# Delta-rule groups: the second sweep of the solve's level one moves between the halves of the third projection, and VectorE's corner copy moves ahead of y's turn and the sum of squares

## The reference, cut to what matters

```python
qkvz = x @ W_qkvz                       # q, k, v, z of all heads
qkv = silu(causal_conv1d(q | k | v))    # four taps along the tokens
attn = -(k_beta @ k.T * decay_mask)     # strictly lower triangle, chunk by chunk
...                                     # row by row: attn becomes (1 - attn)^-1
value_corrected = attn @ v_beta
for c in chunks:
    v_prime = v_c - k_cumdecay_c @ state
    out     = (q_c @ state) * ge_c + intra_c @ v_prime
    state   = state * gel_c + (k_c * kd_c).T @ v_prime
core = rmsnorm(core * silu(z)); out = core @ W_out
```

## Time and profile before

| | |
|---|---|
| median of 3 runs | 1669.9 us (1666.23 to 1676.31) |
| the profiled execution | 1677.4 us, of which 1675.6 us is the span from first to last instruction |
| PE busy in the span | 84% |
| DVE, ACT, POOL busy | 69%, 49%, 47% |
| the delta rule's 16 groups | from about 560 us to 1550 us of the span |

### The profile page before, as it was taken

One profiled execution on the slowest core, in us unless ns is written; L12 is line 12 of the kernel. 1 busy time (PEld: TensorE's weight loads), 2 busy tenths in 40 slices (PEclk: granted clock), 3 DMA queues, 4 the chain that ended last, 5 costly groups with the idle time before them and its releaser, 6 DMA issues. The chain is left out here.

```text
span 1675.6 us, 38381 instructions
## 1 busy us (share of the span) xinstructions
PE 1406.2 (84%) x14345; PEld 999.1 (60%) x14345; DVE 1156.0 (69%) x2350; ACT 822.9 (49%) x2163; POOL 782.8 (47%) x1118
## 2 busy tenths in 40 slices
PE   5988994189545899999999999999999999976675
PEld 2543342066422567777777677777777777765465
DVE  6887126923475788888888788888887888833623
ACT  3334871043132466665665565665665666632122
POOL 5100000177213366467567467566566566543443
PEclk9999996589877999999999899999999999987788
DMA  8200005066723464565565464654555555331884
GB/s 280 74 2 2 2 1 157 1 199 211 256 58 66 114 148 122 149 177 125 160 156 131 128 160 122 162 153 144 139 157 148 119 160 148 99 107 57 241 253 130
DMA packets 249433, 218.72 MB, mean 131 GB/s; under 512 B 88770, under 2 KB 224962, under 8 KB 247200
## 3 DMA queue, kind: packets, MB, share of 16 engines
q1 hardware_dynamic: 234992, 192.41, 42.7%
q0 software_dynamic: 5712, 15.60, 2.8%
q10 hardware_dynamic: 8544, 8.26, 1.6%
HBM read 133.85 MB, written 82.25 MB: 129 GB/s over the span
## 5 line engine op out<-in xcount | busy, mean ns | idle before, releaser
L1825 DVE SCALAR_TENSOR_TENSOR d_conv<-d_big,all_cw,d_conv 128x1023 f32<-128x1023 f32 (+2 forms) x192 | 245.4, 1278 | 45.6 <-ACT d_conv L2067 43.6
L1547 PE MATMUL d_big<-all_xn_t,all_w 128*128 128x512 f32 x512 | 252.6, 624 | 18.7 <-DVE d_conv L1825 11.9
L1547 PEld LDWEIGHTS d_big<-all_xn_t,all_w 128*128 128x128 f32 x512 | 93.8, 198 | 101.4 <-issue 88.2
L2166 ACT COPY d_ys<-d_big 128x128 f32<-128x128 f32 x256 | 61.0, 266 | 177.7 <-PE d_big L1715 139.8
L2301 POOL TENSOR_TENSOR d_y<-d_y,all_xn 128x256 f32<-128x256 f32 x128 | 96.9, 757 | 107.3 <-DVE d_y L1977 89.5
L1753 PE MATMUL d_big<-all_wo,d_yt 128*128 128x256 f32 x512 | 125.5, 391 | 13.8 <-DVE d_yt L1902 13.8
L2258 POOL TENSOR_TENSOR d_vs<-d_vs,d_sv 128x1024 f32<-128x1024 f32 x32 | 61.2, 1912 | 135.6 <-DMA d_vs<-turned_v_scratch 134.3
L1686 PE MATMUL d_big<-all_w,all_xn_t 128*128 128x256 f32 x512 | 122.6, 383 | 0.0
L1753 PEld LDWEIGHTS d_big<-all_wo,d_yt 128*128 128x128 f32 x512 | 96.9, 197 | 26.3 <-issue 14.4
L1876 DVE SCALAR_TENSOR_TENSOR d_AI<-d_big,d_b_col,d_decay 128x256 f32<-128x256 f32 x256 | 104.3, 474 | 2.0 <-PE d_big L1560 1.2
L1686 PEld LDWEIGHTS d_big<-all_w,all_xn_t 128*128 128x128 f32 x512 | 93.7, 190 | 17.7 <-issue 7.2
(11 more groups left out here) (436 smaller groups left out, 3483.2 us busy)
## 6 DMA issues: line engine op xcount, KB each, us to landing
turned_kq_scratch<-d_turned SPq DMA_DIRECT2D x32, 512.0 KB, 3.8
d_kq_tok<-turned_kq_scratch SPq DMA_DIRECT2D x128, 128.0 KB, 3.1
turned_v_scratch<-d_vs SPq DMA_DIRECT2D x16, 1024.0 KB, 4.1
d_vs<-turned_v_scratch SPq DMA_DIRECT2D x64, 256.0 KB, 5.6
grouped_y_scratch<-d_yx SPq DMA_DIRECT2D x32, 512.0 KB, 3.7
d_yx<-grouped_y_scratch SPq DMA_DIRECT2D x128, 128.0 KB, 3.1
all_w<-in_L_attn_W_qkvz SPq DMA_DIRECT2D x16, 768.0 KB
l_hold<-in_L_ffn_gate_up_proj SPq DMA_DIRECT2D x48, 192.0 KB, 3.5
```

Of the source, the lines that this page charges most:

```text
L1547: mm = pe.matmul(big[0][:, c, :], w_sb[par][:, k, n * DK:(n + 1) * DK], xn_t[:, k, c * 512:(c + 1) * 512], start=(k == 0), stop=(k == KD - 1))
L1825: dve.scalar_tensor_tensor(conv[:, sh:T], src[:, 0:T - sh], cw[:, bass.ds(g, 1), COLUMN_OF[j], 3 - sh], conv[:, sh:T], ALU.mult, ALU.add). ...
```

## The change

Two steps change their place, nothing else: the same instructions with the same waits are issued. On TensorE the second half of projection 2 moves from ahead of `l1y` to behind it. On VectorE `l1y` moves from behind `y_turn` and `ksum` to ahead of both.

```diff
 PE_ORDER
     2; prev iv 7; ... gates 3, l1p 0, l1p 1, l1p 2, l1p 3; next proj 2
-    0, proj 2 1; this l1y 0, l1y 1, l1y 2, l1y 3; next products 0; this l2p; next products 1; this l2py; next products 2;
+    0; this l1y 0, l1y 1, l1y 2, l1y 3; next proj 2 1, products 0; this l2p; next products 1; this l2py; next products 2;
 DVE_ORDER
-    3; this l1p, l0x 2; next kq_turn 1; prev y_turn 0; next ksum; this l1y; next kb; this l2p; next products 0, products 1; ...
+    3; this l1p, l0x 2; next kq_turn 1; this l1y; prev y_turn 0; next ksum, kb; this l2p; next products 0, products 1; ...
```

More of the change, by code:

```diff
@@ L1219 @@
     kq_turn 0; prev gather 6; this l0p; next shift, tap 1 1; prev gather 7; next tap 1 2; this l0x 0, l0x 1; next tap 1
-    3; this l1p, l0x 2; next kq_turn 1; prev y_turn 0; next ksum; this l1y; next kb; this l2p; next products 0, products 1; this l2y; next products 2;
+    3; this l1p, l0x 2; next kq_turn 1; this l1y; prev y_turn 0; next ksum, kb; this l2p; next products 0, products 1; this l2y; next products 2;
     this state 0, gather 0, r 1; next products 3; this state 1, gather 1; next tap 2 1; this r 2; next tap 2 2; this
```

## The result

The changed kernel takes 1698.8 us (median of four runs) against 1672.6 of the kernel before, run beside it (four runs). One of the four, at 1718.9, lies apart from the other three (1690.0 to 1699.3) and is left out of the ratio, which is 1.0137 [1.0099, 1.0174]. The change is slower, by 26 us between the medians and 23 by the ratio, where 1668.3 us was forecast, 1.6 us faster. The profiled execution took 1690.0 us, the lowest of the four, so its trace shows only part of the loss.

What follows compares the result with a forecast made beforehand. TensorE was taken to bound each group (59.66 of 61.00 us busy). Gains of 0.7 and 2.5 less a 1.6 us collision made 1.6 us less than the 1669.9 median: 1668.3 us, range 1661 to 1676.

Steps and rivals of the forecast that it cites:

- TensorE's instruction supply: Rival in sweep `l1y`: issue stalls of 1.9 us in each second group, 8 x 1.9 less 3.2, 1682 us; chance 0.03.
- 0.38 will remain: Ordinary groups: with `kb` 0.27 us later, `vs` still starts 0.38 us behind `kxb`'s start, instead of 0.65.
- One collision more: Group 3: `kxb`, 0.27 us later, falls inside GpSimd's `vs` and is held; cost 1.6 us.
- Slower: `kb` runs into `vs`: Rival: VectorE's later `kb` collides with GpSimd's `vs`; 8 collisions give 1678.7 us, all thirteen groups 1686; chance 0.07.
- In groups 0, 6, 10 and 14 TensorE itself was late in `l1y`, or VectorE waited for it: nothing.: Term for four groups where the copy did not hold TensorE up: no gain and no loss counted.
- the 0.12 us per ordinary group: L1936 starts 0.12 us sooner as `half_p` no longer waits for the copy; six groups, 0.7 us gained.
- the cover of 0.02: Ahead of L1936: `half_p` ends late enough to hide the later `kb`, by 0.02 us.
- The late transposes of groups 4, 8 and 11: Late `y_turn` held the corner copy there; with the copy ahead, gains of 0.70, 0.58 and 0.58 us.
- what the prediction left to group 15: Last group, copy directly behind TensorE: 0.64 of its 1.51 us wait taken as gain.
- what the prediction left open: Port rule: only two-input or two-port VectorE operations are hit, so transpose `y_turn` would be free; no row settles it.

Runs made afterwards that it cites:

- run 3: Changed kernel with 58 semaphore increments added once at the head of TensorE's first projection; 1.0210 of the kernel before.
- run 6: Changed kernel with 58 TensorE semaphore increments per group and 20 once, so blocks end at the sweep's 26th instruction; 1.0052 of the kernel before.
- run 7: Changed kernel with 58 TensorE semaphore increments per group and 152 once, so blocks end at the sweep's 150th instruction; 1.0393 of the kernel before.
- run 11: The changed kernel once more, nothing altered, for a second trace; 1.0143 of the kernel before.
- run 12: run 6 with one wait more: GpSimd starts `vs` only when the next group's `kb` is done; 1667.1 us, 0.9957 of the kernel before.
- run 2: Kernel before with VectorE's half of the change alone, TensorE's order as before; 1.0489 of the kernel before.
- run 4: Changed kernel with VectorE's `y_turn` behind `ksum` and `kb` instead of ahead of them; 1.0071 of the kernel before.
- run 10: Kernel before with 58 TensorE semaphore increments per group and 6 once, nothing else; 1.0050 of the kernel before.

## Why the prediction was wrong, by its steps

**The rival that came true, and was argued away.** "TensorE's instruction supply" was named, with the very mechanism (what parts `l1y` from `l1p` shrinks from 3.7 to 1.9 us), and got 0.03, "against it: fourteen groups show next to none". That is the first step that failed; in the sum itself the term stood at nothing. Two stops in sixteen groups were read as rare chance. They stand where a block ends late in the sweep, and a stop of 0.12 us in a third group was one too. A sweep that comes sooner makes them more and longer: run 1, with TensorE's half alone, has 11.7 us of them. Runs 3, 6, 7 and 11 show that block ends set the places; the size, 7.5 us in the first trace and 9.1 in run 11, is about half of that rival's 15.2.

**"0.38 will remain."** The second step that failed. `kb` came 0.39 later, not 0.27: the corner copy starts 1.51 behind `kq_turn`, with its wait of 0.26, where `y_turn` had started 1.17 behind it. In the group shown `vs` also came 0.21 sooner against `kq_turn`. The 0.38 us that were to remain in an ordinary group were 0.05 there. One collision more was counted, 1.6 us; long operations of `kb` went from 4 to 9 (13 in run 11), the wait for L1936 from 2.4 to 7.4 (11.8). "Slower: `kb` runs into `vs`" was the other rival, at 0.07. By itself it costs 0.95% (run 12 against run 6).

**Two rivals as if they were independent.** "In groups 0, 6, 10 and 14 TensorE itself was late in `l1y`, or VectorE waited for it: nothing." Before, VectorE made `y_turn` and `ksum` while it waited for a late sweep. Now they stand behind the corner copy, and `kb` comes 2.3 us later than it did (1.12 + 1.21), into a `vs` that waits for a DMA and not for them. No sentence of the prediction asked what stands behind the corner copy when the copy is late. Group 6 of the trace of before had shown it: a stop, and two operations of `kb` held behind it.

```profile
935.52 0.26 PE L1622 MATMUL d_big<-d_Y,d_P 32*32 32x32 f32 x2 [2.92 <-issue]
...
936.71 1.66 DVE L1847 TENSOR_SCALAR d_ek<-d_ss 128x8 f32<-128x8 f32 x1
...
938.64 1.72 DVE L1851 TENSOR_TENSOR d_b_col<-l_cols,d_rk 128x16 f32<-128x16 f32 x1
```

Runs 2 and 4 show the link: with the sweep late in every group `kb` is held in every group, and with `kb` moved ahead of `y_turn` it is held behind stops alone. Whether stops and collisions together cost more than their sum is not shown, since the runs that have one of them hold different parts of the change and of the increments.

**The clock.** No term of the prediction has it. Behind stops and long waits TensorE runs at 0.50 for a while, which makes up most of the 9.2 us of added busy time in the first trace and of the 14.5 in run 11.

**What was right.** L1931 stands directly behind L1886 with an idle of 0.26 released by L1625, and TensorE's wait for it fell from 3.4 to 0.9 over all 16 groups. `half_p` starts 0.17 sooner. Group 3's collision came, and TensorE waited 1.7 us for it, where 1.6 was counted. But of the 0.12 us per ordinary group next to nothing was left at L1936 (5.46 for 5.48), because `kb`, not `half_p`, now ends last ahead of it: the cover of 0.02 that the prediction named was gone. The late transposes of groups 4, 8 and 11 cost nothing any more, and the 0.9 us that are left are what the prediction left to group 15 (1.51 less 0.64).

**Where page and trace meet.** The Trainium skill, page "Runtime: NRT & Kernel Launch", section "Instruction fetch mechanics", says that an engine's instructions come in blocks of 16 KiB, 256 instructions, the next fetched while the current one runs, at a cost that is mostly hidden. The trace agrees on the blocks (29,425 instructions in 115 packets of 16 KB, and places that move by 58) and not on what is hidden: 11.3 us of stops in this kernel's sweep, 33.6 in run 7.

The Trainium skill, page "SBUF — State Buffer", section "SBUF: two separate sides", says that VectorE's operation and GpSimd's lock each other out for a whole instruction, if VectorE's has two SBUF inputs or a two-port mode. The trace agrees: L1847 and L1851 end within 0.03 us of a `vs` instruction. It also settles what the prediction left open: L1838, which ran beside the same `vs` in group 10, took 1.18 us as ever, and L1902, which began 0.04 us behind the start of `vs` in group 6, took 1.25.

**Open.** Why a packet of instructions starts when it does, and so why a stop lasts 0.4 us in one group and 4.1 in another; what sets the start of `vs` from run to run; most of run 10; and what share of the 0.4% of run 12 is the change's own.

## What to carry to other kernels

A stall by "issue" in few groups is not rare chance until its places have been numbered: count the instructions of a period modulo 256, and ask in which periods a block ends late in a dense run of small matmuls before making that run come sooner. Before an operation is moved behind another on its queue, ask what happens to it when that other is late, not only when it is on time. Two engines that keep apart by 0.4 us of luck may be better kept apart by a wait: one semaphore on GpSimd was worth 0.95% here.

## What the runs showed of the hardware that was not expected

- Where a block of 256 TensorE instructions ends late in a dense sweep of 32x32 matmuls, TensorE stands for 0.4 to 4.1 us (the changed kernel), until 1.2 to 1.8 us behind the end of the next block's packet (60 stops in 14 traces); 132 instructions more, issued once, made 57 us (runs 6 and 7).
- Beside a `vs` of GpSimd (1.95 us an instruction), TENSOR_SCALAR 128x8 and TENSOR_TENSOR 128x16 on VectorE are held to its end (0.54 and 1.72 us instead of 0.17 in group 10); RECIPROCAL 128x8 (0.20), TENSOR_REDUCE (1.18) and STREAM_TRANSPOSE (1.25 in group 6) are not.
- After a stop of 2.86 us the granted clock of a stretch was 0.50, and four projection matmuls took 2.71 us instead of 1.98; over whole traces TensorE's added busy time is about half of the time at 0.50.
